# A graph convolution and expert kernel: a third late chunk, spans of three and four slots mixed, pair steps spread over slots

## What is computed

```python
def _gcn_layer(x, W, b, src, dst, norm, n_nodes):
    xt = x @ W
    msg = xt[src] * norm[:, None]
    agg = jax.ops.segment_sum(msg, dst, num_segments=n_nodes)
    return jax.nn.relu(agg + b)
...
deg_out = jax.ops.segment_sum(edge_weight, src, num_segments=N_NODES)
deg_in = jax.ops.segment_sum(edge_weight, dst, num_segments=N_NODES)
norm = edge_weight * jax.lax.rsqrt(deg_out[src] * deg_in[dst] + EPS)
h6 = _gcn_layer(h5_all, W6, b6, src, dst, norm, N_NODES)
h7 = _gcn_layer(h6, W7, b7, src, dst, norm, N_NODES)
out = h7 @ Wp + bp
```

## Time and profile before

| | |
|---|---|
| median of 3 runs | 3160.35 us (3156.64 to 3161.22) |
| the profiled execution | 3165.63 us, span 3163.6 us |
| busy: PE, DVE, ACT, POOL | 2643.9, 1907.9, 860.6, 1969.9 us |
| mean granted clock of TensorE | 0.918 |
| layer 1's gathers | 374.0 to 1522.3 us |
| layer 2's gathers | 1552.0 to 2641.1 us |
| first expert block | 2682.2 us |

### The profile page before, as it was taken

How to read it: one execution, slowest core, us unless ns; L and a number is a source line. 1 busy time by engine, 2 the same in 40 slices (tenths; PEclk the granted TensorE clock), 3 DMA queues, 4 the chain that set the end, 5 groups by cost and what they waited for, 6 DMA issues and landing times. The chain is left out here.

```text
span 3163.6 us, 54052 instructions
## 1 busy us (share of the span) xinstructions
PE 2643.9 (84%) x16919; PEld 2017.8 (64%) x16919; DVE 1907.9 (60%) x6028; ACT 860.6 (27%) x2052; POOL 1969.9 (62%) x1932
## 2 busy tenths in 40 slices
PE   4567479999999999987598988888988875899994
PEld 3456247676667666664376766666666652889984
DVE  9999878888888878875104544555545447532210
ACT  5677711122122222113100100000100001556652
POOL 0000277777777777777477757777777773467663
PEclk8699789999999999998799989999999985999998
DMA  4001355666665656668666756666666773344444
GB/s 129 0 22 43 113 161 187 201 203 204 199 203 188 191 183 202 204 198 291 200 201 217 261 189 199 220 224 222 224 222 216 219 234 94 60 64 72 70 69 113
DMA packets 221697, 530.81 MB, mean 168 GB/s; under 512 B 42025, under 2 KB 131934, under 8 KB 218238
## 3 DMA queue, kind: packets, MB, share of 16 engines
q0 software_dynamic: 102336, 252.47, 31.0%
q1 hardware_dynamic: 89582, 175.97, 15.7%
q10 hardware_dynamic: 29520, 99.17, 8.5%
HBM read 377.61 MB, written 156.24 MB: 169 GB/s over the span
## 5 line engine op out<-in xcount | busy, mean ns | idle before, releaser
L983 POOL DMA_INDIRECT arena<-table,src_i x1712 | 1680.6, 982 | 589.5 <-issue 515.6
L2116 PE MATMUL bank<-arena 128*128 128x257 f32 x4900 | 1245.5, 391 | 1.9 <-ACT zcd L1790 1.2
L2116 PEld LDWEIGHTS bank<-arena 128*128 128x128 f32 x4900 | 901.0, 194 | 204.0 <-issue 85.8
L2101 PE MATMUL bank<-arena 128*128 128x294 bf16 x2352 | 425.6, 295 | 49.2 <-DVE arena L1301 32.3
L1329 DVE TENSOR_TENSOR arena<-arena,bank 128x294 f32 x784 | 357.3, 456 | 178.7 <-PE bank L2101 166.7
L1301 DVE SCALAR_TENSOR_TENSOR arena<-iota_f,arena 128x256 f32<-128x256 f32 x784 | 366.7, 468 | 0.0
L2101 PEld LDWEIGHTS bank<-arena 128*128 128x128 bf16 x2352 | 226.7, 100 | 207.0 <-DVE arena L1329 46.2
L2129 PE MATMUL bank<-arena,s_all 128*32 128x257 f32 x3424 | 254.4, 419 | 87.7 <-DMA arena<-table,src_i 79.8
L1777 ACT COPY arena<-zero 128x2144 f32<-128x2144 f32 (+1 forms) x104 | 156.2, 1533 | 398.2 <-DMA chunks<-arena 335.7
L1009 POOL DMA_INDIRECT acc<-arena x105 | 178.4, 1699 | 126.2 <-ACT arena L1906 96.6
L1300 DVE TENSOR_SCALAR arena<-iota_key,arena 128x294 bf16<-128x294 bf16 x784 | 242.6, 309 | 0.0
...
...
## 6 DMA issues: line engine op xcount, KB each, us to landing
...
arena<-table,src_i POOLq DMA_INDIRECT x1712
zsum<-zc SPq DMA_DIRECT2D x107, 128.5 KB, 3.5
...
arena<-in_W ACTq DMA_DIRECT2D x16, 512.0 KB, 16.1
...
```

The source lines that it names most:

```text
L983: pool.indirect_dma_start(gat[:, r, j, 0:D], None, table[L], bass.IndirectOffsetOnAxis(ap=src_i[:, col:col + 1], axis=0)).then_inc(gathere ...
L2101: last = pe.matmul(ps_b[t % len(ps_b)], halves[:, t % OH_RING, word, :, half], ohk[:, t % OH_RING], start=(i == 0), stop=(i == 2))
L2116: last = pe.matmul(ps_ap, adj[:, c % 2, h, 0:P], xp[:, h], start=(h == 0), stop=(h == XB_ALL - 1))
```

## The change

It builds and stores one more late chunk, so that layer 2 sums 816 tiles densely (27 chunks) and has 100 groups; layer 1 keeps its 110 groups and 24 applied chunks.

- `LATE_CT` is (31, 31, 18), built in turns 0 to 3, 4 to 8 and 9 to 12. Chunk 24 is stored in turn 5, 25 in turn 10, both by ScalarE; ScalarE zeroes the buffer for chunk 26 in turn 8; SP stores chunk 26 after layer 1. Layer 2 uses the buffers the other way round, and chunk 0 is loaded in turn 12 (7 before).
- Chunks 0 to 4 and every later one with number 0 or 2 modulo 5 span three slots, the others four: 94 slots in all, for 27 chunks.
- The bounds that say when the rows of a pair are complete are tighter (`chunks_for`, `groups_for`). Pair starts are now 10, 16, 19, 23, 26, 30, 34, 37, 42, 45, 50, 55, 58, 62, 66, 70, 74, 77, 84, 87, 91, 94, 97, 100, 103; the pair that needs both chunk rows and group rows is 12, not 11. The lists are counted at slot 97, copied at 99, blocks begin at slot 100; 18 blocks stand beside pairs, as before.
- In layer 1 pair 23 is handled in turn 12, and only pair 24 after the last turn. In a turn TensorE's `combine` and ScalarE's `copy_rows` come after the first pair of the turn instead of after all.
- A pair's steps in layer 2: on TensorE the projection moves from the end of stage 0's slot to the front of the next, `pair_T` to the end of stage 0's slot, the list matmuls to the front of their slots; on VectorE stage 0 of a pair is done before the other pair's stage, the one-hots of the first tile in stage 3, of the second in stage 4; on ScalarE the relu comes after the row copies.
- The scratch area in SBUF is smaller by 280 words a partition; rows of three pairs (not two) are zeroed at the start.

```diff
@@ -32,11 +32,11 @@
 DT = LONG_CHUNKS * LONG_CT + (CHUNKS - LONG_CHUNKS) * CT
-LATE_CT, SHORT = (18, 30), 8
+LATE_CT, SHORT = (31, 31, 18), 5
 ALL = CHUNKS + len(LATE_CT)
...
 N_CHUNKS = CHUNKS, ALL
-SPANS = [3] * SHORT + [4] * (ALL - SHORT)
+SPANS = [3 if c < SHORT or c % 5 in (0, 2) else 4 for c in range(ALL)]
 CHUNKS_END = sum(SPANS)
@@ -44,17 +44,20 @@
-MERGED_PAIRS = 11,
+MERGED_PAIRS = 12,
+ROW_TILES = 3
...
-BLOCKS, LATE_PAIRS, ZERO_PAIRS, PER_SLOT = 105, 3, 2, 2
+BLOCKS, LATE_PAIRS, ZERO_PAIRS, PER_SLOT = 105, 3, 3, 2
...
+
+L2_WORDS = 3640
...
@@ -582,12 +579,12 @@
-        EXTRAS = [range(DT + LATE_CT[0] * k // FIRST_EXTRA, DT + LATE_CT[0] * (k + 1) // FIRST_EXTRA)
-                  for k in range(FIRST_EXTRA)]
-        EXTRAS += [range(DT + LATE_CT[0] + LATE_CT[1] * k // 8, DT + LATE_CT[0] + LATE_CT[1] * (k + 1) // 8)
-                   for k in range(8)]
+        LATE_TURNS = FIRST_EXTRA, 5, 4
+        EXTRAS = [range(chunk_start(CHUNKS + i) + LATE_CT[i] * k // n, chunk_start(CHUNKS + i) + LATE_CT[i] * (k + 1) // n)
+                  for i, n in enumerate(LATE_TURNS) for k in range(n)]
...
-        FIRST_STORED_AT, FIRST_LOADED_AT = FIRST_EXTRA + 1, FIRST_EXTRA + 3
+        STORED_AT = FIRST_EXTRA + 1, sum(LATE_TURNS[:2]) + 1
+        ZEROED_AT, FIRST_LOADED_AT = sum(LATE_TURNS[:2]) - 1, TAIL - 2
@@ -608,10 +605,19 @@
-            return next(c for c in range(ALL) if chunk_start(c) >= tiles_before((b + 1) * PT * P) + CT // 2)
+            return next(c for c in range(ALL) if chunk_start(c) >= tiles_before((b + 1) * PT * P) + ROW_TILES)
...
-            return min(2 * ceil_div(tiles_before((b + 1) * PT * P) + 2 * TG - G0[L] * TG, 2 * TG), GROUPS[L])
+            return min(2 * ceil_div(tiles_before((b + 1) * PT * P) + (2 * TG if L else TG) - G0[L] * TG, 2 * TG),
+                       GROUPS[L])
+
+        LATE_PAIR = LOOP_PAIRS + 1
+        TURNS = TAIL - TAIL_FROM - 2
+        TAIL_PAIR_COUNT = LATE_PAIR - EARLY_PAIRS
+        TAIL_PAIRS = [range(0)] * TAIL_FROM + [range(EARLY_PAIRS + TAIL_PAIR_COUNT * k // TURNS,
+                                                     EARLY_PAIRS + TAIL_PAIR_COUNT * (k + 1) // TURNS)
+                                               for k in range(TURNS)] + [range(LATE_PAIR, NPAIR - 1), range(0)]
+        assert LATE_PAIR == NPAIR - 2 and groups_for(0, LATE_PAIR) == GROUPS[0] - 2
@@ -651,7 +657,7 @@
-        COPIED_AT = LISTED_AT + 3
+        COPIED_AT = LISTED_AT + 2
...
@@ -871,20 +877,28 @@
                         load_stored()
+                    if k == TAIL - 1:
+                        store_table(LATE_PAIR)
+                    if k % 2 == 0:
+                        store_group(0, LOOP_GROUPS + k)
                     for b in TAIL_PAIRS[k]:
+                        if b == LATE_PAIR:
+                            load_early(b)
                         if b + 2 < LATE_PAIR:
...
                             store_table(b - 1)
-                    store_group(0, LOOP_GROUPS + k)
-                for b in range(LATE_PAIR, NPAIR):
-                    load_early(b)
-                for b in range(LATE_PAIR - 1, NPAIR):
-                    store_table(b)
+                        if k % 2 and b == TAIL_PAIRS[k][0]:
+                            store_group(0, LOOP_GROUPS + k)
+                    if k % 2 and not TAIL_PAIRS[k]:
+                        store_group(0, LOOP_GROUPS + k)
+                load_early(NPAIR - 1)
+                store_table(NPAIR - 1)
                 sp.wait_ge(onehot_made, DTA)
...
                 carry_chunk(1, 0)
+                sp.wait_ge(chunk_stored, stores_until(ALL - 1))
                 sp.wait_ge(added, DTA)
@@ -1506,8 +1520,9 @@
                     places(i, b, slot)
                     first_output(i)
-                if s >= 4:
-                    one_hots(i, s - 4)
+                    one_hots(i, 0)
+                if s == 4:
+                    one_hots(i, 1)
             def layer2_slot(n, c, j, g, stages):
@@ -1522,7 +1537,7 @@
                     block_rows(0, 2 * LOADED)
-                for i, b, s in stages:
+                for i, b, s in sorted(stages, key=lambda stage: stage[2] > 0):
                     pair_stage(i, b, s, i % 2, i // 2, i - 1 if i > 1 else None)
@@ -1693,8 +1708,7 @@
-                for b in range(LATE_PAIR, NPAIR):
-                    tail_pair(b)
+                tail_pair(NPAIR - 1)
@@ -1820,7 +1834,7 @@
-            def tail_pairs(pairs):
+            def tail_pairs(pairs, n):
@@ -1829,6 +1843,10 @@
                         pair_out(b - 1)
+                    if b == pairs[0]:
+                        copy_rows(0, n)
+                if not pairs:
+                    copy_rows(0, n)
@@ -1870,7 +1888,8 @@
                 for i, _, s in stages:
-                    stage_of(i, s)
+                    if s:
+                        stage_of(i, s)
                 for j in js[1:]:
@@ -1878,6 +1897,8 @@
                         half_tanh(i)
+                    if s == 0:
+                        stage_of(i, s)
                 if c and c + 1 < ALL and first_of_chunk:
@@ -1913,11 +1934,11 @@
             def load_chunk(c):
-                for rows, part in chunk_pieces(c, c % 2):
+                for rows, part in chunk_pieces(c, (c + 1) % 2):
                     act.dma_start(part, rows).then_inc(chunk_in[c % 2], 16)
...
             def load_first(c):
-                act.wait_ge(chunk_stored, stores_until(CHUNKS + c + 1))
+                act.wait_ge(chunk_stored, stores_until(CHUNKS + c + 2))
                 load_chunk(c)
...
@@ -2012,15 +2035,20 @@
                         zero_behind(CHUNKS - 1, 3)
-                    if k == FIRST_STORED_AT:
-                        act.wait_ge(added, DT + LATE_CT[0])
-                        for rows, part in chunk_pieces(CHUNKS, CHUNKS % 2):
+                    if k in STORED_AT:
+                        c = CHUNKS + STORED_AT.index(k)
+                        act.wait_ge(added, chunk_start(c + 1))
+                        for rows, part in chunk_pieces(c, c % 2):
                             act.dma_start(rows, part).then_inc(chunk_stored, 16)
+                    if k == ZEROED_AT:
+                        act.wait_ge(chunk_stored, stores_until(CHUNKS + 1))
+                        for i in range(SLICES):
+                            zero_chunk(ALL - 1, *slice_bounds(i))
                     if k == FIRST_LOADED_AT:
                         load_first(0)
-                    tail_pairs(TAIL_PAIRS[k])
-                    copy_rows(0, n)
-                tail_pairs(range(LATE_PAIR, NPAIR))
+                    tail_pairs(TAIL_PAIRS[k], n)
+                pair_root(NPAIR - 1)
+                pair_relu(0, NPAIR - 1, b6c)
                 pair_out(NPAIR - 1)
@@ -2113,7 +2141,7 @@
-                    last = pe.matmul(ps_ap, adj[:, c % 2, h, 0:P], xp[:, h], start=(h == 0), stop=(h == XB_ALL - 1))
+                    last = pe.matmul(ps_ap, adj[:, (c + L) % 2, h, 0:P], xp[:, h], start=(h == 0), stop=(h == XB_ALL - 1))
@@ -2230,23 +2258,25 @@
+            def stage_begin(i, s):
+                if s == 1:
+                    project(i, 1, wp, ps_proj)
+                if s >= 4:
+                    list_tile(i, s - 4)
+
             def stage_first(i, slot, s):
-                if s == 0:
-                    pair_T(1, i, slot)
                 if s == 2:
-            def stage_last(i, s):
+            def stage_last(i, slot, s):
                 if s == 0:
-                    project(i, 1, wp, ps_proj)
+                    pair_T(1, i, slot)
                 if s == 2:
...
                     second_bias(i)
-                if s >= 4:
-                    list_tile(i, s - 4)
@@ -2256,6 +2286,11 @@
                     sums(1, g)
+                for i, _, s in stages:
+                    stage_begin(i, s)
+                if n == COPIED_AT:
+                    close_list()
+                    reopen_list()
                 if j == 0 and c is not None:
@@ -2267,13 +2302,10 @@
                 for i, _, s in stages[:1]:
-                    stage_last(i, s)
+                    stage_last(i, i % 2, s)
                 for i, _, s in stages[1:]:
                     stage_first(i, i % 2, s)
-                    stage_last(i, s)
-                if n == COPIED_AT - 1:
-                    close_list()
-                    reopen_list()
+                    stage_last(i, i % 2, s)
...
@@ -2384,11 +2420,12 @@
                             apply_step(0, CHUNKS - 1, step)
-                    for b in TAIL_PAIRS[k]:
+                    for b in TAIL_PAIRS[k][:1]:
                         tail_pair(b)
                     combine(0, n)
-                for b in range(LATE_PAIR, NPAIR):
-                    tail_pair(b)
+                    for b in TAIL_PAIRS[k][1:]:
+                        tail_pair(b)
+                pair_T(0, NPAIR - 1, (NPAIR - 1) % 2)
                 project(NPAIR - 1, 0, w7, ps_f(NPAIR - 1))
...
```

26 lines of the change are left out of this document (14 added, 12 removed).

## The result

The changed kernel ran in 3174.0 us (median of 7 runs, 3165.4 to 3182.7) beside 3156.6 for the kernel before on the same chip: a ratio of 1.0054, 95% interval 1.0037 to 1.0071. It is a little slower; the forecast was 3110. The profiled run took 3174.98 us with a span of 3173.1, so 9.5 us more than the span before.

What follows compares the result with a forecast made beforehand. It took GpSimd's gathers and TensorE, slowed by pair waits, to bound layer 2 together. Setup +1, layer 1's end -3.6, layer 2 -36, end -14 and blocks +3 gave -50 us: median 3110, range 3080 to 3146.

Steps and rivals of the forecast that it cites:

- TensorE is the bound: Rival, chance 0.10: the new order removes no TensorE waits in layer 2, so the change is slower, +15 us, median 3172.
- Layer 2 up to the last chunk: Layer 2, first sums to last chunk's sums: 21.1 us more TensorE work against 57 us saved, -36 us.
- the scaling: Layer 2 pair transposes waiting for VectorE's scaling: 28 of 35.1 us would go, bounds 0 and 35.
- Chunk transfers: Late chunk's store and chunk 0's load near layer 1's end: done 45 us ahead of first use, cost 0.
- The order's own terms: Layer 2 pair steps reordered: scaling 28, relu 16.7, one-hots 15.3, norms -8, clock 5, net 57 us of 108 saved.
- the gathers' floor: GpSimd's gather pace limits layer 2: at most -63 us there; as a rival, chance 0.12, median 3083.
- The clock: TensorE in layer 2 keeps its faster clock when it idles less: 5 us saved; the cited rule allowed up to 62.
- The new chunk: One more chunk for TensorE in layer 2: 23.5 us added, 2.4 us of sums taken away, +21.1 us.
- Layer 1's end: Everything up to layer 2's first gather, with setup, added tiles and pair 23's move: -2.6 us.
- Moving pair 23: Pair 23 put into layer 1's last-but-one turn: layer 2's first gather comes 5.6 us sooner.
- the tiles: 32 more tiles in layer 1's last turns, mostly hidden under GpSimd's gathers: +2 us, bounds 0 and +23.
- The end and the blocks: Last chunk's sums to first expert block: -14 us, bounds -25 and 0; expert blocks: +3, 0 to +8.

Runs made afterwards that it cites:

- e1: Kernel before with only the new order of the pair steps, 26 chunks and 104 groups kept: ratio 0.9847 to the kernel before, 3110.8 us.
- e3: Changed kernel with each layer 2 chunk load issued in the chunk's second slot instead of its first: ratio 0.9963 to the kernel before.
- e4: Changed kernel with layer 2 chunk loads from the third chunk on cut to one of seven column blocks, output wrong: ratio 0.9857 to the kernel before.
- e7: Changed kernel with layer 2's pairs, all but the last dense one, started one slot later: ratio 0.9995 to the kernel before.
- e9: e1 with each layer 2 chunk load issued in the chunk's second slot instead of its first: ratio 0.9900 to the kernel before.
- e6: Changed kernel with all of pair 23's layer 1 steps put back behind the last turn: ratio 1.0012 to the kernel before.
- e5: Changed kernel with VectorE's two one-hot instructions per tile from tile 784 on replaced by one short one, output wrong: ratio 1.0059 to the kernel before.
- e8: Changed kernel with the third late chunk's 18 tiles built behind pair 24 instead of in layer 1's last turns: ratio 1.0056 to the kernel before.

## Why the prediction was wrong, point by point

**The range missed** (3080 to 3146 for 3174), and the time is near that of the rival "TensorE is the bound" (3172; its own sum of +15 gives 3175), but not by its mechanism: that one had the order save nothing because stage 2 took back all, and e1 shows the order alone saving 48 us. That the number fits is luck. The order was forecast rightly and what came with it wrongly.

**Layer 2 up to the last chunk, -36 forecast, +2.4 measured.** The failed step is the scaling: "of the 35.1 us I take 28", with the remark that single waits "were for rows that a store had to land first". I priced the order of the steps on VectorE and TensorE and not the slots in which the pairs start. The change moves them next to chunk loads, and TensorE waited 39.5 us for the scaling instead of 7; e3, e4, e7 and e9 show the price of that place: 19 to 62 us in after, by the edit, and 17 in the order-alone kernel. Two more terms were off in after as in e1: the list's waits, 20.7 us where none was to be left, and the norms' 20.1 more where I took 8. Working out the pair starts from `SPANS` and `ROW_TILES` beside the chunk starts, before any run, would have shown it.

**Chunk transfers, 0 forecast.** I asked whether a chunk comes in time, found 45 us to spare and closed the case; I never asked who waits behind it. The rule that I cited against this place, the Trainium skill's "DMA: Bandwidth & Descriptors", section "Issuing engines are not separate DMA queues", was the right one and I used it for the wrong transfer: loads of ScalarE and SP interleave on the same 16 DMA engines, and the trace agrees, 14.2 us to the scaling with the chunk load's bytes in front and 4.5 us with a seventh of them.

**The order's own terms.** Measured alone (e1): 44.7 us in place of 57. Scaling 33 of 35 us (28 forecast), relu 16.7 (16.7), but the list's one-hots -4.5 in place of +15.3: its 8 longer waits became 20 short ones. The norms took 24.5 back, forecast 8 with a bound of 25. The clock, 5 us forecast from the sums alone, gave 27 (892.8 to 866.1 us busy for as many matmuls, at 0.93, e1 at 0.96), 19 of them in the projection. The second rule that I cited, the Trainium skill's "TensorE: Matmul & The Clock Gate", section "What's actually happening", pointed this way, and the trace agrees in direction; the row lies between my 5 us and the 62 that I had estimated by it. Two errors of opposite sign hid each other, and the gathers' floor capped the sum.

**The new chunk, +21.1 forecast.** Its matmuls took 627.9 us for 611.6, +16.3 and not +23.5. TensorE's whole work there rose by only 1.7: the projection, which I had not counted as work, took 44.6 us for 59.7, and the list's matmuls 40.0 for 34.4. The chunk's term was 7 us too high, and a term for the moved projection was missing.

**Layer 1's end, -2.6 forecast, +27.1 measured.** Two steps failed. Moving pair 23 was priced as a chain of 5.6 us getting shorter; e6 shows that it costs 10 us net, since the last group's sums then wait for its rows. And the tiles were weighed against GpSimd's pace ("a VectorE that was busy 44.4 of 80"): the turns need not only keep that pace, they have to make up a delay. At group 104 the sums were 15 us behind its last gather in the kernel before, 23 in e6 and 26 in after. The turns that follow decide what is left of that: before, the sums of groups 104 to 108 came 7.9 us apart while the gathers took 10.3, and the last ones stood 5 us behind (1527.2 for 1522.3). In e6 they came 11.0 us apart, and the last ones were 18 us behind (1539.0 for 1520.8). That is the 13 us that e6 leaves. TensorE over these four turns, before and in e6, with the columns of the windows above:

```profile
1485.90:1517.30 31.40, 26.89 (x189) 18.58 (x188) 19.63 (x66) 13.34 (x40) 24.06 (x25) 1.00 0.86 269
...
1493.00:1537.10 44.10, 33.84 (x213) 22.11 (x212) 29.27 (x97) 19.46 (x45) 21.21 (x22) 0.92 0.75 233
```

It had 6.9 us more of work, and stood 5.8 us more. So TensorE isn't full, and more work is only half of it. Apart from pair 23's turn, the delay grew most in two turns, those in which ScalarE stores a finished late chunk of 3.4 MB. From group 101 to 102, behind chunk 24's store, it grew by 13.0 us in after, 12.7 in e6 and 7.3 before; from 106 to 107, behind chunk 25's, by 4.6 in after and 5.0 in e6, where the kernel before has no such store and made up 2.3. In after, the first of them and the rows of a pair that SP asked for at 1458.1:

```profile
1452.75 3.61 ACTq L2042 DMA_DIRECT2D chunks<-arena  x7
...
1468.76 0.17 DVE L1373 TENSOR_SCALAR din<-zrow 128x2 f32<-128x2 f32 x1 [10.65 <-DMA zrow<-zsum]
...
1469.94 3.78 PE L2196 MATMUL bank<-w,hT 128*128 128x256 f32 x8 [9.30 <-ACT hT L1825]
```

It looks like the loss of layer 2 again, a pair's rows behind a bulk transfer. My "Cost 0" had the second store begin at 1482 us, and it was issued at 1517.7. All this is read from traces only. e5 and e8 failed to win the 13 us back, and both left the stores where they are. No run moved a store, so what they cost, and which edit would help, stays open.

**The end and the blocks.** -21.3 for -14, inside its bounds; +1.2 for +3. The chain there is as told: TensorE stands 13.2 us for ScalarE behind its expert loads, then come the norms.

**The better kernel** is e1, the order without the third late chunk: 1.5% faster than before and 2.1% than after.
